# One more product of a two-level Strassen feed-forward kernel cut into seven, in two of four groups

## What is computed

```python
W = weights[condition]                          # (64, 64, 64): one 64x64 matrix per batch row
y = einsum('bct,bcd->bdt', x, W)                # x is (64, 64, 1024)
xf = y.reshape(4096, 1024)
scores = xf @ Wr.T                              # 64 experts
G = softmax over the 16 largest scores, 0 elsewhere
h = einsum('nd,krd->nkr', xf, A)                # 4096 x 1024 x (64*16)
out = x + 2 * einsum('nkr,kdr->nd', h * G[:, :, None], B)
```

## Time and profile before

| | us |
|---|---|
| median of 3 runs | 707.08 (707.0 to 707.63) |
| the profiled execution, whole | 707.46 |
| its span in the profile | 705.7 |
| PE busy in it | 700.4 |
| DVE busy in it | 568.8 |
| ACT busy in it | 292.2 |
| second stage of group 2 (its Q2 to Q3) | 455.2 to 543.4 |
| second stage of group 3 | 628.2 to 702.2 |

### The profile page before, as it was taken

One profiled execution on the slowest core, in us unless ns is written; L12 is line 12 of the kernel. 1 busy time (PEld: TensorE's weight loads), 2 busy tenths in 40 slices (PEclk: granted clock), 3 DMA queues, 4 the chain that ended last, 5 costly groups with the idle time before them and its releaser, 6 DMA issues.

```text
span 705.7 us, 11098 instructions
## 1 busy us (share of the span) xinstructions
PE 700.4 (99%) x3822; PEld 608.5 (86%) x3822; DVE 568.8 (81%) x1022; ACT 292.2 (41%) x541; POOL 15.8 (2%) x22
## 2 busy tenths in 40 slices
PE   8999999999999999999999999999999999999998
PEld 8888888888888888988999888898899988888897
DVE  5888998897757899889795867987668496699885
ACT  5575554534535541444333542242334364233220
POOL 0000000100000000010000000001000000000100
PEclk9999999999999999999999999999999999999999
DMA  8976679787899998979989775868769987666886
GB/s 314 405 291 279 211 281 401 229 261 268 332 382 417 415 359 290 406 255 325 388 312 412 285 271 189 301 247 245 248 274 372 380 311 258 199 217 211 228 329 239
DMA packets 68937, 212.35 MB, mean 301 GB/s; under 512 B 10706, under 2 KB 13394, under 8 KB 68242
## 3 DMA queue, kind: packets, MB, share of 16 engines
q1 hardware_dynamic: 64802, 204.30, 78.0%
q0 software_dynamic: 2304, 4.20, 3.9%
q10 hardware_dynamic: 1776, 3.15, 1.2%
HBM read 150.80 MB, written 65.01 MB: 306 GB/s over the span
## 4 chain that ended last, share of the span: by engine, by line
PE 99%; DMA 1%; DVE 0%; issue 0%; DVEq 0%
PE Pb L755 40%; PE Pb L788 29%; PE Pb L809 13%; PE Cb L737 8%; PE S L852 4%; PE Pb L831 3%; DMA xc<-in_wts 1%; PE S L844 1%; PE T L907 0%; PE T L913 0%; PE Pb L771 0%; PE Cb L866 0%; PE S L866 0%; PE T L866 0%; DVE Q L1212 0%
## 5 line engine op out<-in xcount | busy, mean ns | idle before, releaser
L755 PE MATMUL Pb<-Op,Wt 128*128 128x512 f32 x888 | 214.2, 391 | 0.0
L755 PEld LDWEIGHTS Pb<-Op,Wt 128*128 128x128 f32 x888 | 165.4, 188 | 33.9
L788 PE MATMUL Pb<-Wt,Op 128*128 128x512 f32 x744 | 179.7, 391 | 0.0
L788 PEld LDWEIGHTS Pb<-Wt,Op 128*128 128x128 f32 x744 | 138.1, 188 | 28.1 <-DVE Op L1212 0.4
L1212 DVE TENSOR_TENSOR Q<-Pb,Q 128x512 f32<-128x512 f32 (+1 forms) x105 | 92.8, 901 | 27.9 <-issue 17.5
L1212 DVE TENSOR_TENSOR Op<-R,Op 128x512 fp32r<-128x512 f32 x100 | 66.6, 686 | 23.4 <-ACT Op L945 23.3
L755 PE MATMUL Pb<-Ox,Wt 128*128 128x512 f32 x300 | 75.3, 390 | 0.0
L998 ACT COPY R<-Cb 128x512 f32<-128x512 f32 x60 | 35.1, 587 | 91.2 <-PE Cb L737 91.2
L755 PEld LDWEIGHTS Pb<-Ox,Wt 128*128 128x128 f32 x300 | 56.0, 188 | 11.5
L945 ACT CAST Op<-R 128x512 fp32r<-128x512 f32 x100 | 58.3, 622 | 17.3 <-DVE R L1212 10.4
L1212 DVE TENSOR_TENSOR Cq<-Pb,Cq 128x1024 f32<-128x1024 f32 (+1 forms) x46 | 44.5, 966 | 24.3 <-issue 10.4
(11 more groups left out here) (118 smaller groups left out, 688.9 us busy)
## 6 DMA issues: line engine op xcount, KB each, us to landing
Wt<-Wd SPq DMA_DIRECT2D x201, 512.0 KB, 6.5
Wd<-Wt SPq DMA_DIRECT2D x56, 512.0 KB, 5.1
xc<-in_x SPq DMA_DIRECT2D x24, 512.0 KB, 5.4
Q<-in_x SPq DMA_DIRECT2D x16, 512.0 KB, 5.3
out<-Q SPq DMA_DIRECT2D x8, 1024.0 KB, 4.8
BR<-in_B SPq DMA_DIRECT2D x4, 1024.0 KB, 8.5
Q<-in_x SPq DMA_DIRECT2D x16, 256.0 KB, 5.6
out<-in_x SPq DMA_DIRECT2D x16, 256.0 KB, 5.9
```

What stands on the lines that cost most here:

```text
L755: t = e.matmul(Pb[:, j, :], Wt[:, k, a, 128 * c:128 * c + 128], part((USES1[m], s, c), z), start=fresh and (c, a, z) == (0, 0, 0), stop=(c ...
L788: t = e.matmul(Pb[:, i, :], part((USES2[m], s, c), a)[:, 128 * i:128 * i + 128], Wt[:, k, z, :], start=fresh and (c, a, z) == (0, 0, 0), s ...
```

## The change

`TWO` takes product 5 (Q5) in for groups 2 and 3, so that Q4, Q5 and Q3 are all made of sub-products there. Q5 takes the banks of `BANK1` ([3, 0, 3, 2, 3, 2, 3]). Its sub-products are not put into `Q`: ScalarE copies sub-products 0, 2, 3 and 6 into `Cq[:, 0]`, VectorE adds 1, 4 and 5 to that (`drain_five`), and then each half of `Cq[:, 0]` is added to Q5's quarter and to Q3's quarter of `Q` (`add_five`, two additions of 128 x 1024 for each of two halves). Half 1 is added at the end of Q5's step 6, half 0 at the start of Q3's step 0, ahead of the drain of Q3's sub-product 0. Q5's operand S1 is split in seven forms instead of four, with four more sums (`sum_five`), made during Q4 in group 2 and during Q7 in group 3. The sum of B from which its seven weights are made is stored in DRAM in group 0 (`T1b`, two stores of 512 KB), loaded in group 2's first stage, and the seven weights are made and stored there.

```diff
@@ -20,10 +20,10 @@
 SENT = -3.4028234663852886e38
 
 
-TWO = [(), (0, 4, 6), (0, 4, 6), (0, 4, 6)]
+TWO = [(), (0, 4, 6), (0, 4, 5, 6), (0, 4, 5, 6)]
 
 ONE = (2, 3)
-LEVEL = (4, 6, 0, 7)
+LEVEL = (4, 6, 0, 7, 5)
 
 USED = [[*(range(56 + 7 * LEVEL.index(7), 63 + 7 * LEVEL.index(7)) if s in ONE else range(4)), *range(4, 28)] +
         [n for m in range(7) for n in (
@@ -55,7 +55,7 @@
 
 MADE = [0, 6, 1, 4, 2, 3, 5]
 MADE_AT = {4: [16, 17, 20, 21, 22, 23, 24], 6: [0, 1, 2, 3, 5, 6, 7], 0: [12, 13, 14, 15, 19, 20, 21],
-           7: [8, 9, 10, 12, 13, 14, 20]}
+           7: [8, 9, 10, 12, 13, 14, 20], 5: [12, 13, 14, 15, 20, 21, 22]}
 
 HEAD = [(0, 0, 0), (0, 0, 1), (1, 0, 0), (1, 0, 1), (2, 0, 0), (0, 1, 0), (1, 1, 0), (2, 0, 1), (3, 0, 0), (2, 1, 0),
         (3, 1, 0), (3, 0, 1)]
...
@@ -138,7 +143,9 @@
     if m == 3 and 4 in TWO[s]:
         return [("G22", k) for k in ((0, 1), (2,), (3,), (4,))[c]]
     if m == 4 and 4 in TWO[s]:
-        return [("G22", c + 5)] if c < 2 else [("S1", c - 2)] if c < 6 else []
+        return [("G22", c + 5)] if c < 2 else [("S1", c - 2)] if c < 6 or 5 in TWO[s] else []
+    if m == 5 and m in TWO[s]:
+        return [("S1", c + 5) if c < 2 else ("S4", c - 2)]
     if m == 5 and 6 in TWO[s]:
         return [("S4", k) for k in ((0,), (1, 2), (3,), (4,))[c]]
     if m == 6 and 6 in TWO[s]:
...
@@ -648,6 +689,14 @@
                         for k in (6, 0):
                             if s == 1 and step - 1 in MADE_AT[k]:
                                 made_store(k, MADE_AT[k].index(step - 1))
+                        if s == 2 and step - 1 in MADE_AT[5]:
+                            made_store(5, MADE_AT[5].index(step - 1))
+                        if (s, step) == (2, 6):
+
+                            e.wait_ge(v_made, 28)
+                            e.wait_ge(l_b[1], 32)
+                            e.wait_ge(l_b[2], 32)
+                            e.dma_start(raws[2], T1b).then_inc(l_b[4], 16)
 
...
+                        if s == 0 and step in (17, 19):
+                            n = (step - 17) // 2
+                            e.wait_ge(v_bsum["T1b"], 2 * n + 2)
+                            e.dma_start(T1b[:, 2 * n:2 * n + 2, :], BR[:, 0, 2 * n:2 * n + 2, :]).then_inc(l_b[1 + n], 16)
                         if s == 0 and m < 6:
...
+                        if 5 in TWO[s] and (m, i) in ((5, 6), (6, 0)):
+                            e.wait_ge(v_out, out_done(s, 5, m == 5, 1))
+                            q_store(s, 2 if m == 5 else 0, 0, 1024)
+                        if m == 5 and m in TWO[s]:
+                            continue
                         if m == 6 and m in TWO[s]:
                             if i in (1, 5, 6):
                                 e.wait_ge(v_out, out_done(s, 6, i))
@@ -797,7 +855,12 @@
                 at = n % NW
                 e.wait_ge(v_lo[USES2[m]], split_done(USES2[m], s, k))
                 e.wait_ge(l_t[at], w_landed(n))
-                if k == 0:
+                if m > 4 and 5 in TWO[s] and k in (0, 1, 3):
+                    if m == 5:
+                        e.wait_ge(v_out, out_done(s, *{0: (3, 3, 1), 1: (4, 1), 3: (4, 5)}[k]))
+                    else:
+                        e.wait_ge(v_out, out_done(s, *{0: (4, 6), 1: (5, 1), 3: (5, 5)}[k]))
+                elif k == 0:
                     e.wait_ge(*((v_prod["P4"], 4 * s + 2) if m == 0 else (v_out, out_done(s, m - 1, 1, 1))))
                 elif k == 3:
                     e.wait_ge(*((v_prod["P4"], 4 * s + 4) if m == 0 else (v_out, out_done(s, m - 1, 2, 1))))
...
                     for c in range(2):
                         for a, z in ((0, 0), (0, 1), (1, 0)):
-                            t = e.matmul(Pb[:, BANK2[k], 256 * i:256 * i + 256],
+                            t = e.matmul(Pb[:, banks_two(m)[k], 256 * i:256 * i + 256],
                                          part((USES2[m], s, k), a)[:, c, 128 * i:128 * i + 128],
                                          Wt[:, at, z, 256 * c:256 * c + 256],
...
-                if k in (0, 1, 3):
+                if k == 0 and 5 in TWO[s - 1]:
+                    e.wait_ge(*in_output(s - 1, 5, 6))
+                elif k in (0, 1, 3):
                     e.wait_ge(v_out, out_done(s - 1, *{0: (5, 3, 1), 1: (6, 1), 3: (6, 5)}[k]))
...
@@ -954,6 +1019,13 @@
                         e.wait_ge(l_b[4], 32)
                 elif n >= 4:
                     e.wait_ge(*stored(m, n - 4))
+                elif m == 5:
+
+                    e.wait_ge(l_b[4], 48)
+                    if n < 2:
+                        e.wait_ge(p_cond, rows_number(2, 6 + n, 0))
+                    else:
+                        e.wait_ge(v_lo["S4"], split_done("S4", 1, 6))
...
@@ -970,6 +1042,8 @@
                     e.wait_ge(p_cond, rows_number(1, 6 + n, 0))
                 else:
                     e.wait_ge(v_wlo, 48 if n < 2 else 52)
+                    if n > 1:
+                        e.wait_ge(l_b[n - 1], 32)
...
+                        elif m == 5 and m in TWO[s] and i in (0, 2, 3, 6):
+                            e.wait_ge(p_two, form_done(s, 5, i))
+                            e.wait_ge(v_lo["S1"], split_done("S1", s, 5))
+                            e.wait_ge(v_ysum, s1sum_done(s, "t4"))
+                            e.copy(five(i), Pb[:, BANK1[i], :].rearrange("p (i n) -> p i n", n=256)).then_inc(a_out, 1)
                         k = cond_step(s, m, i)
                         if k is not None:
                             for a in (1, 0):
...
+
+            def sum_five(s, name):
+
+                (b, to), n = places2(5, s), s1sum_done(s, "t1")
+                if name == "t1":
+                    e.wait_ge(v_s1, 4 * s + 4)
+                    if s + 1 < NS:
+                        e.wait_ge(v_lo["G22"], split_done("G22", s, 5))
+                    else:
+                        e.wait_ge(v_lo["T4"], 4 * s + 4)
+                    add(quarter(to, "t1"), quarter(b, "b12"), quarter(b, "b11"), v_ysum, ALU.subtract)
+                elif name == "t2":
+                    e.wait_ge(v_ysum, n)
+                    add(quarter(to, "t2"), quarter(b, "b22"), quarter(to, "t1"), v_ysum, ALU.subtract)
+                elif name == "t3":
+                    add(quarter(to, "t3"), quarter(b, "b22"), quarter(b, "b12"), v_ysum, ALU.subtract)
+                else:
+                    e.wait_ge(v_ysum, n + 1)
+                    add(quarter(to, "t4"), quarter(b, "b21"), quarter(to, "t2"), v_ysum, ALU.subtract)
+
+            def drain_five(s, r):
+
+                if r in (1, 4, 5):
+                    e.wait_ge(p_two, form_done(s, 5, r))
+                    e.wait_ge(*in_output(s, 5, {1: 0, 4: 3, 5: 2}[r]))
+                    add(five(r), Pb[:, BANK1[r], :].rearrange("p (i n) -> p i n", n=256), five(r), v_out)
+
+            def add_five(s, n):
+
+                D = Cq[:, 0, 2 * n:2 * n + 2, :]
+                if n:
+                    e.wait_ge(v_out, out_done(s, 5, 5))
+                    e.wait_ge(*in_output(s, 5, 3))
+                else:
+                    e.wait_ge(*in_output(s, 5, 6))
+                for name in ("Q5", "Q3"):
+                    tile, half = INTO[name][0] + 2 * n, INTO[name][1]
+                    to = Q[:, tile:tile + 2, 512 * half:512 * half + 512]
+                    e.wait_ge(v_out, out_done(s, {"Q5": 3, "Q3": 2}[name], 2 * n + 1))
+                    add(to, D, to, v_out)
...
@@ -1453,13 +1579,15 @@
                 e.wait_ge(p_two, form_done(s, m, r))
                 if r in (1, 4, 5):
                     e.wait_ge(*in_output(s, m, {1: 0, 4: 3, 5: 2}[r]))
+                elif m == 6 and 5 in TWO[s]:
+                    e.wait_ge(v_out, out_done(s, 5, INTO2[r][1], 2))
                 elif r in (0, 6):
                     e.wait_ge(v_out, out_done(s, m - 1, 1, 1))
                 else:
                     e.wait_ge(v_out, out_done(s, m - 1, 3, 1))
                 to = out2(m, r)
                 add(to, Pb[:, BANK2[r], :].rearrange("p (i n) -> p i n", n=256), to, v_out)
-                if r == 0 and m:
+                if r == 0 and m and (m != 6 or 5 not in TWO[s]):
...
+                        if s == 2 and step in MADE_AT[5]:
+                            made_lo(5, MADE_AT[5].index(step))
...
@@ -1550,9 +1680,23 @@
                 for m in range(7):
                     for c in range(steps(s, m)):
                         if m in TWO[s]:
-                            drain_two(s, m, c)
+                            if m == 6 and c == 0 and 5 in TWO[s]:
+                                add_five(s, 0)
+                            if m == 5:
+                                drain_five(s, c)
+                            else:
+                                drain_two(s, m, c)
                             for name, k in splits_second(s, m, c):
                                 lo(name, s + (name == "y21"), k)
```

(44 more changed lines are left out.)

20 lines of the change are left out of this document (13 added, 7 removed).

## The result

| | before | changed |
|---|---|---|
| median of 5 runs, us | 707.04 (706.9 to 707.63) | 716.66 (715.67 to 717.87) |
| ratio to before, 95% interval | | 1.0137 (1.0123 to 1.0150) |
| span of the profiled execution, us | 705.7 | 714.9 |
| granted clock over it | 0.999 | 0.995 |

The account below looks back on a forecast made before the run. TensorE, 99% busy and 99% of the chain, was taken as the bound. Savings, small waits and holes summed to +3.9 us in group 2 and +2.9 in group 3, +6.8 on 707.08: 713.9 us, range 711.5 to 717.7.

Parts of the forecast that it names:

- TensorE's own saving: Q5 in groups 2 and 3 goes from 10.89 to 10.07 us each, 1.64 us less in all.
- The hole in group 2: Before Q3's sub-product 2, TensorE waits 4.20 us for VectorE's drain of sub-product 0, behind four additions of 4.56 us.
- T: The end of Q5 on TensorE, from which the forecast counts VectorE's steps at Q3's start.
- The hole in group 3: Before Q3's sub-product 2, TensorE stands 3.24 us instead of 0.14, behind VectorE's four additions.
- The small waits: Waits for VectorE and ScalarE: 0.55 us in group 2's Q4, 0.5 and 0.1 in group 3's Q4 and Q5.
- Nothing for the preparation: Making seven weights in group 2's first stage, with 4.7 MB of transfers, costs nothing; without cover up to 2.7 us.
- The clock: Rival: granted clock falls in the holes, about 1.9 us lost each; one hole 715.8, both 717.7 us; chance 0.25.
- The rival of late weights: Group 2's Q4 to group 3's P2: 28 loads in a row land late, adding 1 to 3 us (716); chance 0.06.
- its weight loads behind them wait with them: SyncE's stores of Q5's rows issue 4 us later, delaying the loads behind; put at nothing, as TensorE stands then too.
- the sums hide, and the kernel is faster: Rival: VectorE reaches Q3's first drain in time, giving 706.6 us, or 705.4 without small waits; chance 0.06.

Follow-up runs that it names:

- quads: Changed kernel with Q5's putting together on VectorE in 128 x 512 pieces at idle moments, operand sums moved, stores later: 706.33 us, ratio 0.9987 to the kernel before.
- quads_old_sums: quads with the four sums of Q5's operand back at the change's steps: 707.3 us, ratio 0.9998 to the kernel before.
- made_only: Kernel before plus only the preparation (T1b and seven weights made and stored, used by nobody): 707.48 us, ratio 0.9999.
- filled2: Changed kernel with matmuls that nothing reads put before Q3's sub-product 2, 17 in group 2 and 13 in group 3: 714.26 us, ratio 1.0101 to the kernel before.
- only2: Changed kernel with Q5 of sub-products in group 2 alone: 712.99 us, ratio 1.0088 to the kernel before.
- thin_adds: Changed kernel with its eight additions of Q5's sum cut from 128 x 1024 to 128 x 8 elements: 708.23 us, ratio 1.0011 to the kernel before.
- thin_late_store: thin_adds with group 2's two 1 MB stores moved to group 3's first stage: 706.49 us, ratio 0.9989 to the kernel before.
- half0_behind: Changed kernel with half 0's two additions behind, not ahead of, the drain of Q3's sub-product 0: 713.34 us, ratio 1.0084 to the kernel before.
- only3: Changed kernel with Q5 of sub-products in group 3 alone, seven weights still made in group 2: 711.0 us, ratio 1.0060 to the kernel before.

## Why the prediction held, point by point

- **TensorE's own saving.** Forecast 0.82 us a product. In quads, where nothing waits in group 2, that group from Q4 to the end of Q3 takes 35.55 us (506.77 to 542.32) after 36.41: 0.86. The Trainium skill's cycle counts (TensorE: Matmul & The Clock Gate, Back-to-back issue gap) had given 1.19; the runs bear out the rows.
- **The hole in group 2.** Forecast: sub-product 2 goes on at T + 7.08, a hole of 4.20. Measured: T + 7.10 (532.72 to 539.82), which is 4.22 past the moment it was due; the profile's idle time is 4.06, since it counts from the modelled end of the matmul before. VectorE's drain began at T + 6.26 instead of T + 6.08, and TensorE followed after 0.84 us instead of 1.00; two small errors that cancel.
- **The hole in group 3.** Forecast T + 6.12 and 3.24; measured T + 6.13 (697.86 to 703.99) and 3.25 by the same count.
- **The small waits.** Forecast 0.55 in group 2's Q4, measured 0.40 (36 matmuls in 4.88 us, in quads in 4.48). Forecast 0.6 for Q4 and Q5 of group 3, measured 0.5 (677.04 to 697.86 is 20.82, less 20.14 and less the 0.14 that was there before). As a pair they are the 1.0 us of quads_old_sums.
- **Nothing for the preparation.** Shown by made_only. By start times from P2 to Q2, group 2's first stage is 84.7 us in the kernel before, the changed one, made_only and quads.
- **The clock.** This is the term that was mis-sized. The sum without it had bounds of 712.0 to 715.4, which do not hold the result; it lies in the stated range only because that range reached out to this rival. (The bounds don't follow from their terms either: 1.15 and 2 x 0.60 us each way, added straight, make 711.6 to 716.3.) I gave it a chance of 0.25 and left it out of the forecast; in the profiled execution it fell in one of two holes and cost 2.6 us, and the median of 716.66 lies between my price for one hole (715.8) and for both (717.7). The mechanism was right, by filled2. The price was low for this execution: I read 1.9 us from the warm-up's 3.83 us, and here the clock stayed at half for almost 6 us of work. In only2 it cost 1.6. My reading that it falls 2.15 us after TensorE stops did not hold as a rule: after the last matmul in front of a hole it took 3.2 us in the changed kernel, 5.3 in only2, and in group 3's hole of 3.10 us it did not fall at all in the traced execution.
- **The rival of late weights.** I had the mechanism, "its weight loads behind them wait with them", and put it at nothing because TensorE stands in that time too. That cover was real, and it goes with the holes: then the place of the two stores costs 1.2 us in P2 (thin_adds), 1.6 us in all (thin_adds against thin_late_store). So my rival "the sums hide, and the kernel is faster" at 705.4 to 706.6 lacked a condition: short sums alone give 708.2, and it takes the stores out of the way as well to come to 706.5 (thin_late_store) or 706.3 (quads).

What stays open: the rest of quads' shortfall against 705.7. Its end, 0.45 us longer behind TensorE's last matmul, is one part; no run took it away.

## What to carry to other kernels

Before a product is cut finer, list on the draining engine everything that stands ahead of the first drain whose bank is used again, and compare its sum with the time until TensorE is back at that bank: here 4.56 us of additions against 1.88 us, for a gain of 0.82 us. Sums put together apart need not go in one piece, nor soon: a piece can go as soon as its part is complete, or one product later, and its store with it. When a hole goes, look again at what it covered: a term that was put at nothing because the engine stands there anyway is due again. A store that waits for its data holds back every load issued behind it on the same queue.

## What the runs showed of the hardware

- A hole of 4.06 us in TensorE's work brought the granted clock from 1.00 to 0.50 (from 2.4 to 1.2 GHz), in the changed kernel inside the hole, some 3.2 us after the last matmul, and in only2 5.3 us after it, with work already going on. It came back 5.8 us after work went on in the first and 4.6 us in the second, which cost 2.6 and 1.6 us. A hole of 1.79 us did it too (half0_behind). With a hole of 3.10 us the clock stayed at 1.00 in both traced executions (the changed kernel, only3), while other executions of only3 had 0.997 and 0.995 over the run and took up to 2.4 us longer.
- Matmuls that nothing reads, 17 of them in 4 us, kept it at 1.00, and each was recorded as two.
- A GpSimd addition of 128 x 1024 from SBUF took 2.77 us, and one VectorE addition with two SBUF inputs beside it took 2.8 to 2.9 us instead of 0.68.
- Two stores of 1 MB ahead of weight loads in SyncE's queue, waiting for VectorE, put off a load's issue from 1.5 to 4.4 us after its place was free, and its landing time grew from 6.0 to 7.6 us (thin_late_store, thin_adds). Over all loads issued in 530 to 556 us the longest landing grew from 8.0 to 13.2 us; the load that took 13.2 was issued at 547.9, and no matmul waited for it.
